# A two-layer graph kernel: packing steps one tile later, counting steps spread over the column, one mark moved

## The reference

```python
h = jnp.maximum(_layernorm(x, axis=-1), 0.0)
# layer 0
x1 = swish((adj @ h) @ W0 + b0)
x  = x + swish((adj @ x1) @ W0 + b0)
# layer 1
h = jnp.maximum(_layernorm(x, axis=-1), 0.0)
a_hat = adj + jnp.eye(8192)
d = jnp.sum(a_hat, axis=1) ** (-0.5)
x = x + (a_hat * d[:, None] * d[None, :] @ h) @ W1.T + b1
```

## Time and profile before

| | |
|---|---|
| median of 3 runs | 1447.41 us (1445.41 to 1447.41) |
| the profiled execution's own time | 1448.34 us |
| its span, first to last instruction | 1444.9 us |
| mean granted TensorE clock | 0.994 |
| TensorE busy | 1384.5 us, 96% |
| VectorE busy | 1011.8 us, 70% |
| ScalarE busy | 684.1 us, 47% |
| read from memory | 322.44 MB |

### The profile page before, as it was taken

One profiled execution on the slowest core, in us unless ns is written; L12 is line 12 of the kernel. 1 busy time (PEld: TensorE's weight loads), 2 busy tenths in 40 slices (PEclk: granted clock), 3 DMA queues, 4 the chain that ended last, 5 costly groups with the idle time before them and its releaser, 6 DMA issues.

```text
span 1444.9 us, 18304 instructions
## 1 busy us (share of the span) xinstructions
PE 1384.5 (96%) x6598; PEld 649.3 (45%) x6598; DVE 1011.8 (70%) x2334; ACT 684.1 (47%) x781; POOL 33.9 (2%) x30
## 2 busy tenths in 40 slices
PE   3778999999999999999999999999999999999998
PEld 1333444444444444444444454454444444444444
DVE  7978888899988786786774777877565555546331
ACT  7788878788777667656560112222311221132000
POOL 1100000000000000000000011101000000000000
PEclk9999999999999999999999999999999999999999
DMA  9999999999999898886760111111433233333000
GB/s 378 358 413 408 409 410 403 401 399 399 395 376 387 320 356 318 331 365 263 296 273 29 37 51 66 67 52 62 178 124 146 110 132 137 134 118 123 23 15 24
DMA packets 56255, 335.49 MB, mean 232 GB/s; under 512 B 6240, under 2 KB 6752, under 8 KB 18272
## 3 DMA queue, kind: packets, MB, share of 16 engines
q1 hardware_dynamic: 49104, 322.20, 56.7%
q10 hardware_dynamic: 7056, 12.06, 2.2%
HBM read 322.44 MB, written 11.80 MB: 231 GB/s over the span
## 4 chain that ended last, share of the span: by engine, by line
PE 78%; DMA 10%; DVE 8%; issue 3%; ACT 2%; DVEq 0%; ACTq 0%; SPq 0%
PE acc_ps L586 21%; PE acc_ps L587 21%; DMA ring<-adj 9%; PE acc_ps L527 9%; PE acc_ps L528 9%; PE early_ps L496 6%; PE early_ps L497 6%; PE z_ps L479 3%; DVE marks L843 2%; PE kept_ps L505 2%; PE kept_ps L506 2%; ACT marks L662 1%; DVE stats L822 1%; ACT unused L707 1%; DVE node_a L836 1%
## 5 line engine op out<-in xcount | busy, mean ns | idle before, releaser
L707 ACT ACTIVATE unused<-ring 128x2048 uint8<-128x2048 uint32 x220 | 420.0, 1909 | 92.3 <-DMA ring<-adj 82.4
L527 PE MATMUL acc_ps<-marks,node_a 128*128 128x512 fp8e4 x1024 | 392.0, 383 | 52.7 <-DVE node_a L836 31.2
L528 PE MATMUL acc_ps<-marks,node_a 128*128 128x512 fp8e4 x1024 | 392.1, 383 | 1.8 <-issue 1.8
L586 PE MATMUL acc_ps<-ring,node_a 128*128 128x512 fp8e4 x1024 | 388.1, 379 | 0.0
L587 PE MATMUL acc_ps<-ring,node_a 128*128 128x512 fp8e4 x1024 | 388.1, 379 | 0.0
L843 DVE TENSOR_SCALAR marks<-ring 128x2048 uint8<-128x2048 f32 x226 | 277.0, 1226 | 70.7 <-DMA ring<-adj 41.5
L343 DVE TENSOR_SCALAR ring<-bits 128x256 uint32<-128x256 uint32 (+1 forms) x784 | 159.3, 276 | 89.6 <-PE acc_ps L587 89.5
L527 PEld LDWEIGHTS acc_ps<-marks,node_a 128*128 128x128 f16 x1024 | 100.9, 98 | 188.8 <-issue 74.4
L748 ACT ACTIVATE nT<-acc_ps 128x512 f32<-128x512 f32 x16 | 9.6, 597 | 313.3 <-PE acc_ps L587 313.3
L496 PE MATMUL early_ps<-marks,node_b 128*128 128x512 fp8e4 x416 | 157.7, 379 | 0.0
L497 PE MATMUL early_ps<-marks,node_b 128*128 128x512 fp8e5 x416 | 157.7, 379 | 0.0
(11 more groups left out here) (117 smaller groups left out, 1107.3 us busy)
## 6 DMA issues: line engine op xcount, KB each, us to landing
ring<-adj SPq DMA_DIRECT2D x256, 1024.0 KB, 7.5
marks<-adj SPq DMA_DIRECT2D x36, 1024.0 KB, 5.0
node_b<-x SPq DMA_DIRECT2D x4, 1024.0 KB, 13.0
xch<-x SPq DMA_DIRECT2D x16, 256.0 KB, 2.8
xn_scratch<-xnew ACTq DMA_DIRECT2D x16, 256.0 KB, 2.0
xch<-xn_scratch SPq DMA_DIRECT2D x16, 256.0 KB, 2.9
out<-xnew ACTq DMA_DIRECT2D x16, 256.0 KB, 2.0
part_scratch<-stage ACTq DMA_DIRECT2D x13, 256.0 KB, 5.1
```

Source lines behind the costliest of these rows:

```text
L527: nc.tensor.matmul(acc_ps[c % 2][:, :], hi_of(node_a16, j), byte, start=(j == 0), stop=False)
L528: last = nc.tensor.matmul(acc_ps[c % 2][:, :], lo_of(node_a16, j), byte, start=False, stop=(j == NB - 1))
L586: nc.tensor.matmul(into[:, :], hi_of(node, j), byte.bitcast(E4), start=opens, stop=False)
L707: nc.scalar.activation(unused[:, :], slot(g).bitcast(U32), ACT.Sign, accum_out=nz_count[:, g:g + 1]).then_inc(counted, 1)
```

## The change

Nothing is computed otherwise. VectorE's operations stand at other places in its program:

- the three packing steps of a group stand one tile later each: `pack_half(r)` after tile 4r + 4 instead of 4r + 3, `pack_again(r)` after 4r + 5 instead of 4r + 4, `pack_last(r)` after 4r + 6 instead of 4r + 5; the last group's first step moves behind the loop,
- the eleven counting steps stand at tiles 2, 3, 5, 6, 7, 9, 11, 11, 11, 13 and 15 instead of 2 to 12, and `count_columns` at tile 15 instead of 13,
- `kept_unpack` stands at tile 3 instead of 4,
- the norm is cut into its statistics and its chain, and the mark of tile 8 stands between the two in the fourth norm (at tile 6) instead of at tile 8.

```diff
-COUNT_FROM = 2
-KEPT_UNPACK_AFTER = 4
+KEPT_UNPACK_AFTER = 3
+
+COUNT_AFTER = (2, 3, 5, 6, 7, 9, 11, 11, 11, 13, 15)
+COUNT_OUT_AFTER = 15
...
-            first_norm(0)
-            first_norm(1)
+            for part in range(2):
+                first_stats(part)
+                first_rest(part)
...
-                    if g not in ACT_MARKED:
+                    if g not in ACT_MARKED and g != 8:
                         mark(g)
                     if c == 0 and i % 2 == 0:
                         h_low(i // 2)
-                    if c == 0 and i in (2, 6):
-                        first_norm(2 if i == 2 else 3)
-                    if i % GT == 0 and g > 0:
+                    if g == 2:
+                        first_stats(2)
+                        first_rest(2)
+                    if g == 6:
+                        first_stats(3)
+                        mark(8)
+                        first_rest(3)
+                    if i % GT == 0 and r > 0:
+                        pack_half(r - 1)
+                    if i % GT == 1 and r > 0:
                         pack_again(r - 1)
-                    if i % GT == 1 and g > 1:
+                    if i % GT == 2 and r > 0:
                         pack_last(r - 1)
-                    if i % GT == GT - 1:
-                        pack_half(r)
...
-                    if c >= 1 and COUNT_FROM <= i < COUNT_FROM + COUNT_STEPS:
-                        count_one(c - 1, i - COUNT_FROM)
-                    if c >= 1 and i == COUNT_FROM + COUNT_STEPS:
+                    for step in range(COUNT_STEPS):
+                        if c >= 1 and i == COUNT_AFTER[step]:
+                            count_one(c - 1, step)
+                    if c >= 1 and i == COUNT_OUT_AFTER:
                         count_columns(c - 1)
...
             last = NC * GC - 1
+            pack_half(last)
             pack_again(last)
```

More of the change, by code:

```diff
@@ L816, in _, with norm_stats @@
         def _(dve):
-            def norm(sems, arrived, part, a, n, scale):
-                stat, step, ready = sems
-                s = slice(a, a + n)
+            def norm_stats(stat, arrived, a, n):
                 dve.wait_ge(arrived, 16)
@@ L823, in norm, with norm_rest @@
                 last.then_inc(stat, 1)
+            def norm_rest(sems, part, a, n, scale):
+                stat, step, ready = sems
+                s = slice(a, a + n)
                 dve.wait_ge(stat, part + 1)
@@ L829, in norm, with first_stats, first_rest @@
                 nc.vector.scalar_tensor_tensor(nmr[:, s], twice_mean, -0.5, rstd[:, s], ALU.mult, ALU.mult).then_inc(ready, 1)
-            def first_norm(part):
-                norm((ln_stat, ln_step, ln_ready), x_in[part], part, sum(NORM_PARTS[:part]), NORM_PARTS[part], H_SCALE)
+            def first_stats(part):
+                norm_stats(ln_stat, x_in[part], sum(NORM_PARTS[:part]), NORM_PARTS[part])
+            def first_rest(part):
+                norm_rest((ln_stat, ln_step, ln_ready), part, sum(NORM_PARTS[:part]), NORM_PARTS[part], H_SCALE)
             def h_low(part):
@@ L1191, in general @@
                 for q in range(4):
-                    norm((G.ln_stat, G.ln_step, G.ln_ready), G.x_in[q], q, q * 16, 16, 1.0)
+                    norm_stats(G.ln_stat, G.x_in[q], q * 16, 16)
+                    norm_rest((G.ln_stat, G.ln_step, G.ln_ready), q, q * 16, 16, 1.0)
                 for p in range(3):
```

## The result

| | before | after |
|---|---|---|
| median, runs side by side | 1445.41 us (7 runs, 1444.9 to 1447.41) | 1440.94 us (7 runs, 1440.15 to 1441.8) |
| profiled execution, its own time | 1448.34 us | 1441.80 us |
| its span | 1444.9 us | 1438.7 us |

The ratio is 0.9962, with a 95% interval of 0.9952 to 0.9971: 0.38% faster, about 5.5 us (4.2 to 6.9). The two medians are 4.5 us apart and the means 5.1, both inside that interval. In a later session the changed kernel (`after_again`) gave 0.9965 (0.9951 to 0.9979). The forecast was 1440.0, with 7.5 us to be gained. The time is inside the range; the gain is about three quarters of what the sum said.

The account below looks back on a forecast made before the run. The tile stream, slowed by late VectorE marks, was taken to pace the first 300 us; 1.2 (start) + 5.1 (packing) + 1.70 (TensorE idle) - 0.5 gave 7.5 us, so 1440.0 us, range 1436 to 1446.3.

Parts of the forecast that it names:

- part 1: Packing and counting on VectorE: timely marks recover 85% of the stream's 6.0 us loss to column 5, 5.1 us (2.4 to 6.0).
- the prediction's two signs of being wrong: Step 0 distances still over 41 us with marks on time, or add_bias waits over 2 us in columns 5 to 7.
- Part 2: The start: tile 8's mark at 39.7 us shrinks the stream's 4.0 us hole to about 3; gain 1.2 us (0 to 4.0).
- The sum: At the stall before 231.28: 6.3 us of lead plus 1.70 of TensorE idle time, less 0.5, gives 7.5 us.
- Part 3: The other moves (kept_unpack, pack_last with step 0, count_columns, end of the first phase): 0 us each.
- the slower rival: VectorE reaches add_bias before TensorE's product in columns 5 to 7, delaying loads: 3 us slower, 1450.8; chance 0.06.
- the prediction's other sign of being wrong: Waits of over 2 us at add_bias in columns 5 to 7.
- two points: TensorE's stalls before 231.28, with tiles 6.3 us earlier, and at 316.65, with 11.9; the earlier was taken to decide.
- ring hides: The ring of load slots hides VectorE's lateness, so only the start gains, 1.2 us: 1446.2; chance 0.13.
- ScalarE takes over: ScalarE falls behind in tiles with two jobs and a third of the loss returns: gain 4.1 us, 1443.3; chance 0.12.

Follow-up runs that it names:

- half_late: The kernel before with only pack_half moved to the next tile, 4r + 4: 1443.84 us, ratio 0.9984.
- dose8: The changed kernel with eight more small VectorE operations, each waited for, at tile 3 of columns 2 to 6: 1448.43 us, ratio 1.0026 against the kernel before.
- mark8_only: The kernel before with only the mark of tile 8 moved into the fourth norm: 1445.05 us, ratio 0.9994.
- count_only: The changed kernel's counting steps and kept_unpack at tile 3, with the old packing and mark of tile 8: 1451.21 us, ratio 1.0035 against the kernel before.
- dose3: The changed kernel with three more small VectorE operations, each waited for, at tile 3 of columns 2 to 6: 1441.60 us, ratio 0.9971 against the kernel before.
- pack_only: The kernel before with only the packing steps one tile later; counting, kept_unpack and mark of tile 8 as before: 1442.35 us, ratio 0.9975.
- count_kept4: The kernel before with only the counting steps spread as in the change, kept_unpack staying at tile 4: 1448.74 us, ratio 1.0018.

## Why the prediction was right, and where it was not

**The mechanism of part 1: right.** That the stream paces the first part, that it was not at its rate, that pack_half's wait for ScalarE and the work behind it make VectorE late, and that the packing's move ends this: each was seen in the trace after. half_late shows that the place of pack_half alone brings time, and dose8 that late marks alone cost it.

**Part 1, the size: too high.** The loss up to column 5 was put at 6.0 us, and 85% of it was to come back, 5.1. Back came 164.7 - 160.7 = 4.0, two thirds, and 3.3 in after_again. Counting step 0 of column 5 starts 3.6 us earlier, not 6. The pace of 2.48 us was read where nothing else used the queues. But from column 3 on each column stores its early sums (0.26 MB) at about tile 6, and the four landings around that take 10.5 us instead of 9.9 in columns 4 and 5. These two columns take 40.3 us each, and not 39.7. So part of the "loss" in the earlier trace rows was never lateness. Column 3 gave nothing: from its step 0 to the next it takes 41.45 us (149.99 to 191.44), and took 41.3, though no mark is more than 0.3 us late. This is not the column's own doing: in after_again column 3 takes 40.3 and column 4 takes 41.6. About 1 us more goes in one column or another, and no run tells why. A distance over 41 us with the marks on time was one of the prediction's two signs of being wrong; one of the first six distances shows it. The lateness of the marks of tiles 4 to 10 was put at 1.7 us at most; it is 0.45 in columns 2 to 4, 1.4 in column 5 and 2.5 in column 6.

**Part 2: the size within what can be measured, its way through the stream not shown.** 1.2 us was forecast, 0.9 and 1.3 measured, each with an interval of over 1 us to both sides. The time of the mark (39.82 for 39.7) and TensorE's return (47.04 for 46.9) were as said. The hole became smaller, as said, but came in three pieces up to 58 us: from 40 to 60 us the stream loses 2.6 us against 420 GB/s, and lost 4.2. The sum carried 1.2 us of this on to column 5. The traces don't settle that. Tile 2 of column 1 lands at 68.40 before, at 68.32 in the changed kernel, at 68.89 in after_again and at 66.87 in mark8_only, so single traces differ by more than what is looked for.

**Part 3: right.** No wait of kept_unpack or of step 0 shows. The waits at add_bias that the slower rival spoke of do appear, 1.10, 2.54 and 4.43 us in columns 6, 7 and 8. The 2.54 in column 7 meets the prediction's other sign of being wrong, more than 2 us in columns 5 to 7, but TensorE has no stall at all there, so the wait costs nothing. The stock of marks covered it.

**The sum: right in form, but the lead in it was too large.** At the stall before 231.28 the tiles were to come 6.3 us earlier. That stall was for tile 0 of column 5. ScalarE begins its count of it, on landing, 4.05 us earlier; before and after:

```profile
229.23 1.91 ACT L707 ACTIVATE unused<-ring 128x2048 uint8<-128x2048 uint32 x1 [0.57 <-DMA ring<-adj]
```

```profile
225.18 1.91 ACT L709 ACTIVATE unused<-ring 128x2048 uint8<-128x2048 uint32 x1 [0.57 <-DMA ring<-adj]
```

Its mark starts 4.7 us earlier (225.19, and was 229.91). With the 1.70 us of idle time behind it this gives 5.8 to 6.4 us, and the two spans differ by 6.2. So what was mis-sized is the lead of 6.3 us: in this trace 4.0 of its 5.1 for part 1 came about, and 0.1 of its 1.2 for the start was there in column 1.

The sum also looked at two points only, and a third lies nearly as close. The last stall for a tile is now at 184.49. It answers to the one before at 186.41, on the same tile, which is 1.92 us later. After that TensorE had idle times of 5.2 us before, and has the 1.51 us at 203.83 now: 1.9 + 3.7 = 5.6 us. With the prediction's own leads this point would have given 1.2 + 0.85 x 3.3 = 4.0 us of lead (3.3 us is the loss from column 1 to column 4, 122.3 us for 48 tiles against 119.0) and 3.4 of idle time (5.2 less the 1.81 that stood as "issue" before 206.73, most of which is there after the change too), 7.4 instead of 8.0. So leaving it out accounts for 0.6 us of the error at most. Which point binds also changes from one execution to the next: in after_again the last stall is at 225.59, close to the prediction's point.

**Chances.** The rivals "ring hides" and "slower" are refuted by the time, the first by dose8 too. "ScalarE takes over" had a third of the loss come back; two thirds did. What I did not see is that the change has a harmful half: its counting list is right only with its packing.

**Left open.** TensorE stands still for 1.8 to 3.1 us at tile 5 of column 2 in every trace here but that of dose8 (before 121.06 after, before 124.29 in the kernel before), and for 1.1 to 2.4 us at tile 5 of column 4 in every trace but that of count_only. The tile's mark had been ready for over 2 us when TensorE went on. It is at the same place of the program each time, and no run tells why. After the first of these the granted clock can fall: in the changed kernel's trace it is 0.50, the lower of its two levels, from 120 to 126 us, and matmuls start 0.43 us apart instead of 0.22; in after_again it is not. Both spans are 1438.7, so the slow stretch cost nothing there: TensorE still waits for tiles after it.

## What to carry to other kernels

Work placed on an in-order engine should be spread by what each slot really holds, waits included: a step that waits for another engine belongs one slot later, where its operand is already there, and only then is its old slot free for other work. A ring buffer forgives a little lateness and charges for more, so look at the time from landing to release of each slot and at the rate in fine slices; a DMA share of 1.00 doesn't say that the stream is at its rate. When a stage's pace is read from its best stretch, check that the other users of the queues were there too, and take a lead that arises at the start into the sum only if something downstream keeps it.

## What the runs showed of the hardware

Some operations of VectorE and a conversion on GpSimd get in each other's way. In the changed kernel GpSimd's conversion takes 1.04 us beside the statistics of the norm (38.41), but 3.75 when VectorE goes through a mark, an h_low and a pack_last from 48.74 on without a break. It ends at 52.48, 1.04 us after pack_last does:

```profile
38.41 1.04 POOL L447 TENSOR_SCALAR node_a<-node_b 128x1024 f16<-128x1024 f32 x1 [2.86 <-ACT node_b L670]
43.28 1.07 POOL L447 TENSOR_SCALAR node_a<-node_b 128x1024 f16<-128x1024 f32 x1 [3.83 <-ACT node_b L670]
48.73 3.75 POOL L447 TENSOR_SCALAR node_a<-node_b 128x1024 f16<-128x1024 f32 x1 [4.38 <-ACT node_b L670]
53.61 1.04 POOL L447 TENSOR_SCALAR node_a<-node_b 128x1024 f16<-128x1024 f32 x1 [1.13 <-ACT node_b L670]
```

And VectorE is held up by it: one small operation of the norm's chain takes 0.90 instead of 0.17 us beside the conversion from 43.28, and the mark of tile 12 takes 1.98 instead of 1.23 beside that from 53.61.

```profile
43.48 0.90 DVE L170 SCALAR_TENSOR_TENSOR rstd<-tmp,rstd 128x16 f32<-128x16 f32 x1
44.41 0.17 DVE L168 SCALAR_TENSOR_TENSOR tmp<-rstd 128x16 f32<-128x16 f32 x1
...
53.75 1.98 DVE L850 TENSOR_SCALAR marks<-ring 128x2048 uint8<-128x2048 f32 x1
```

The Trainium skill has this in "SBUF — State Buffer", section "Who interferes with whom": the two engines share a pair of ports, and the one that issues first keeps it for a whole instruction. The rows agree, with 1.07, 0.90, 3.75 and 1.98 us. The sum of the prediction left it out, at 0.7 us a meeting for VectorE; the kernel before has such meetings too.

The ring of four slots has no sharp limit. From the shortest landing it should bear a hold (from a tile's landing to the release of its slot) of 5.2 us, as the prediction says. In column 4 the longest hold of a trace, worked out from the starts of mark and count, and its lowest slice of 1 us from 190 to 230 us are:

| | longest hold, us | lowest slice, GB/s |
|---|---|---|
| after | 2.1 | 377 |
| dose3 | 2.4 | 352 |
| pack_only | 3.0 | 393 |
| count_kept4 | 3.7 | 205 |
| half_late | 3.8 | 287 |
| before | 4.4 | 213 |
| count_only | 4.4 | 147 |
| dose8 | 4.7 | 205 |

Up to about 3 us the rate holds, from 3.7 on it falls, well below 5.2; how deep it falls doesn't follow from the longest hold alone. In column 5 of dose8, with holds up to 6.1 us, one slice has 49. The Trainium skill's fit ("DMA: Bandwidth & Descriptors", "Anatomy of one DMA") would have given 5.5, an estimate. The section gives the fit for single transfers that GpSimd issues, and the loads here are issued by SyncE, up to four at a time; the prediction doesn't say so. As a limit for this ring the runs contradict it.
